# Making the low halves of the expert weights on GpSimd instead of VectorE

## The reference

```
h  = (qk * D / normalizer) v            # per head; D from running sums of log_sigmoid(fg) and ig
x  = x + head_norm(h) * out_w
s  = top2(softmax(layernorm(x) @ gate_w))
x  = x + sum_k s_k * (gelu(xf @ w1[e_k] + b1) @ w2[e_k] + b2)
```

## Time and profile before

| | before |
|---|---|
| time, median of 3 runs | 666.69 us (665.88 to 667.96) |
| profiled execution, span | 672.2 us |
| PE busy | 626.9 us (93%) |
| DVE busy | 489.8 us (73%) |
| ACT busy | 323.3 us (48%) |
| POOL (GpSimd) busy | 187.1 us (28%) |

### The profile page before, as it was taken

One profiled execution on the slowest core, in us unless ns is written; L12 is line 12 of the kernel. 1 busy time (PEld: TensorE's weight loads), 2 busy tenths in 40 slices (PEclk: granted clock), 3 DMA queues, 4 the chain that ended last, 5 costly groups with the idle time before them and its releaser, 6 DMA issues. The chain is left out here.

```text
span 672.2 us, 20373 instructions
## 1 busy us (share of the span) xinstructions
PE 626.9 (93%) x6736; PEld 533.2 (79%) x6737; DVE 489.8 (73%) x1330; ACT 323.3 (48%) x767; POOL 187.1 (28%) x185
## 2 busy tenths in 40 slices
PE   1799998999889899999999999999999999999985
PEld 1567876778677668988989898988889898988774
DVE  2457988979889898985889866757675757666562
ACT  2668888777878746543332232323232323232321
POOL 3000003231323315135345332313141323233112
PEclk9899999969999999999999999999999999999998
DMA  4534537654644636333374423233232323133100
GB/s 139 156 106 148 160 94 231 188 189 144 207 152 137 199 103 208 77 70 78 66 221 93 68 40 61 43 56 46 46 52 44 57 39 64 35 65 53 21 4 1
DMA packets 55036, 66.55 MB, mean 99 GB/s; under 512 B 5472, under 2 KB 50720, under 8 KB 54832
## 3 DMA queue, kind: packets, MB, share of 16 engines
q1 hardware_dynamic: 41552, 48.13, 24.1%
q0 software_dynamic: 13296, 17.32, 14.1%
q10 hardware_dynamic: 112, 0.08, 0.1%
HBM read 41.50 MB, written 24.92 MB: 99 GB/s over the span
## 5 line engine op out<-in xcount | busy, mean ns | idle before, releaser
L1038 ACT ACTIVATE decay_slots<-scores,b_turned 128x256 f32<-128x256 f32 (+1 forms) x312 | 124.4, 451 | 257.4 <-PE scores L1519 244.9
L1519 PE MATMUL scores<-x_slots,w_halves 128*128 128x256 f16 (+1 forms) x1872 | 203.3, 264 | 0.8 <-issue 0.8
L1519 PEld LDWEIGHTS scores<-x_slots,w_halves 128*128 x1872 | 173.4, 98 | 23.3 <-issue 1.4
L641 POOL DMA_INDIRECT expert_rows<-xf_rows,slot_i x64 | 66.7, 1042 | 224.1 <-issue 114.8
L1533 PE MATMUL pv<-w_halves,decay_slots 128*128 x864 | 97.7, 273 | 0.0
L663 POOL DMA_INDIRECT out_rows<-v_centred_and_one,row_ids x36 | 57.8, 1605 | 138.8 <-DVE v_centred_and_one L2111 96.1
L1533 PE MATMUL gate_bank<-w_halves,q_and_k_halves 128*128 x840 | 95.0, 273 | 0.0
L1533 PEld LDWEIGHTS pv<-w_halves,decay_slots 128*128 128x128 f16 x864 | 84.1, 98 | 10.5 <-issue 0.3
L1533 PEld LDWEIGHTS gate_bank<-w_halves,q_and_k_halves 128*128 128x128 f16 x840 | 81.8, 98 | 10.1
L663 POOL DMA_INDIRECT out_rows<-work,row_ids x35 | 55.3, 1580 | 112.1 <-DVE work L2111 84.7
L1257 PEld LDWEIGHTS pv<-v_centred_and_one,decay_slots 128*128 128x128 f32 x512 | 64.5, 197 | 1.6
(11 more groups left out here) (257 smaller groups left out, 845.5 us busy)
## 6 DMA issues: line engine op xcount, KB each, us to landing
weight_stage<-in_L_ffn_w SPq DMA_DIRECT2D x32, 512.0 KB
x_slots<-in_x SPq DMA_DIRECT2D x16, 512.0 KB
weight_stage<-expert_rows SPq DMA_DIRECT2D x30, 272.0 KB
ctx_slots<-in_ctx SPq DMA_DIRECT2D x8, 512.0 KB
out_rows<-x_slots SPq DMA_DIRECT2D x8, 512.0 KB
v_centred_and_one<-expert_rows SPq DMA_DIRECT2D x9, 272.0 KB
expert_rows<-v_centred_and_one SPq DMA_DIRECT2D x9, 272.0 KB
expert_rows<-xf_rows,slot_i POOLq DMA_INDIRECT x64
```

What stands on the lines that cost most here:

```text
L641: pool.indirect_dma_start(table, bass.IndirectOffsetOnAxis(ap=sloti[:, step[1], j, k:k + 1], axis=0), xfn[:, step[1], j, :], None, bounds_ ...
L1038: ins = act.activation(hf[:, f * R:f * R + tr.rows(0)], ps_s[:, q, n * R:n * R + tr.rows(0)], ACT.Gelu, bias=b1T[:, bass.ds(expert, 1), f] ...
L1519: ins = pe.matmul(o, w, xh[:, tr.slot(0) % 2, b, k, 0:tr.rows(0)], start=(n == 0), stop=(n == 3 * KC - 1))
```

## The change

All 32 low halves move from DVE to GpSimd. There a piece takes two instructions: the slot of the stage is multiplied by 64 in place, and, after a wait on a new semaphore for that, the high half is subtracted from it. The semaphore of low halves becomes two, one for each slot of the stage, and SP's loads wait for the one of their slot. The twelve pieces of S0 to S2 stand at the start of GpSimd's list. In a round its list is now: low half 0 of `nxt`, the preparation and the first pair of the scatter of the step before `last`, low half 1, two pairs, low half 2, the last pair, low half 3. So each scatter begins one round later than it did. The scatter of S5 follows behind the loop. DVE's list loses its calls of `weights_low` and is otherwise as it was.

```diff
-        s_lo = sem("weights_low")
+        s_w64 = sem("weights_scaled")
+        s_lo = [sem(f"weights_low{p}") for p in range(2)]
...
-                        sp.wait_ge(s_lo, g * 4 + (n - 1))
+                        sp.wait_ge(s_lo[half], g * 2 + q)
...
-                sp.wait_ge(s_lo, 4 * NSTEP)
+                for done in s_lo:
+                    sp.wait_ge(done, 2 * NSTEP)
...
+                def weights_low(step, n):
+                    g, half, q = number(step), n % 2, n // 2
+                    pool.wait_ge(s_hi, g * 4 + n + 1)
...
+                    src = stage[:, half, :]
+                    pool.tensor_scalar(src, src, W_SCALE, None, ALU.mult).then_inc(s_w64, 1)
+                    pool.wait_ge(s_w64, g * 4 + (n + 1))
+                    pool.tensor_tensor(lo, src, hi, ALU.subtract).then_inc(s_lo[half], 1)
...
                 def body(last, step, nxt, after):
-                    if last is not None:
-                        scatter(last)
+                    older = divmod(number(last) - 1, 2)
+                    weights_low(nxt, 0)
+                    scatter_ready(older)
+                    scatter_row(older, 0)
+                    weights_low(nxt, 1)
+                    scatter_row(older, 1)
+                    scatter_row(older, 2)
+                    weights_low(nxt, 2)
+                    scatter_row(older, 3)
+                    weights_low(nxt, 3)
 
                 def first_steps():
-                    scatter(S0)
+                    for step in (S0, S1, S2):
+                        for n in range(4):
+                            weights_low(step, n)
 
                 first_steps()
                 run_steps(body, pool)
+                scatter(divmod(NSTEP - 3, 2))
...
-                    dve.scalar_tensor_tensor(out=lo, in0=stage[:, half, :], scalar=W_SCALE, in1=hi, op0=ALU.mult,
-                                             op1=ALU.subtract).then_inc(s_lo, 1)
```

More of the change, by code:

```diff
@@ L621, in _, with scatter_row, scatter_ready @@
                     pool.memset(xfn[:, p, :, D:ROW], 0.0).then_inc(s_cp, 1)
-                def scatter(step):
+                def weights_low(step, n):
+                    g, half, q = number(step), n % 2, n // 2
+                    pool.wait_ge(s_hi, g * 4 + n + 1)
+                    e, k = g, q
+                    if half == 0:
+                        hi, lo = (w1s[:, bass.ds(e, 1), a, k, :].rearrange("p a f -> p (a f)") for a in range(2))
+                    else:
+                        hi, lo = (w2s[:, bass.ds(e, 1), a, k * (FC // 2):(k + 1) * (FC // 2), :].rearrange("p a c d -> p (a c d)")
+                                  for a in range(2))
+                    src = stage[:, half, :]
+                    pool.tensor_scalar(src, src, W_SCALE, None, ALU.mult).then_inc(s_w64, 1)
+                    pool.wait_ge(s_w64, g * 4 + (n + 1))
+                    pool.tensor_tensor(lo, src, hi, ALU.subtract).then_inc(s_lo[half], 1)
+                def scatter_row(step, j):
+                    for k in range(2):
+                        if j:
+                            pool.wait_ge(s_sc[step[1]][k], step[0] * SCATTERED + j * 16)
+                            pool.sem_inc(s_held, 1)
+                        pool.indirect_dma_start(
+                            table, bass.IndirectOffsetOnAxis(ap=sloti[:, step[1], j, k:k + 1], axis=0),
+                            xfn[:, step[1], j, :], None, bounds_check=TABLE - 1,
+                            oob_is_err=False).then_inc(s_sc[step[1]][k], 16)
+                def scatter_ready(step):
                     g = number(step)
@@ L635, in scatter @@
                     pool.sem_inc(s_held, 1)
+                def scatter(step):
+                    scatter_ready(step)
                     for j in range(SB):
[L637 to L644, removed]
-                def body(last, step, nxt, after):
-                    if last is not None:
-                        scatter(last)
+                        scatter_row(step, j)
+                def body(last, step, nxt, after):
+                    older = divmod(number(last) - 1, 2)
[8 more added lines that the diff above has]
+                    weights_low(nxt, 3)
                 def first_steps():
-                    scatter(S0)
+                    for step in (S0, S1, S2):
+                        for n in range(4):
+                            weights_low(step, n)
                 first_steps()
                 run_steps(body, pool)
+                scatter(divmod(NSTEP - 3, 2))
                 def add_rows(tr):
@@ L1887, in body @@
                         next_stats(after)
-                    if nxt is not None:
-                        weights_low(nxt, 0)
                     if after is not None:
@@ L1895, in body @@
                         next_a(nxt)
-                        weights_low(nxt, 1)
                         running_max(nxt)
@@ L1901, in body @@
                         h_norm(step)
-                    if nxt is not None:
-                        weights_low(nxt, 2)
                     if step is not None:
@@ L1918, in body @@
                         c_of(nxt, 1)
-                        weights_low(nxt, 3)
                     if nxt is not None and after is None:
@@ L1931, in first_steps @@
                     next_norm(S0)
-                    weights_low(S0, 0)
                     constants()
-                    weights_low(S0, 1)
                     gate_bias(S0)
@@ L1941, in first_steps @@
                     split(S0)
-                    weights_low(S0, 2)
                     max_log_decay(S0)
@@ L1945, in first_steps @@
                     next_stats(S2)
-                    weights_low(S0, 3)
                     c_of(S0, 1)
                     gate_bias(S1)
-                    weights_low(S1, 0)
                     next_norm(S2)
@@ L1954, in first_steps @@
                     c_of(S0, 3)
-                    weights_low(S1, 1)
                     running_max(S1)
                     split(S1)
-                    weights_low(S1, 2)
                     max_log_decay(S1)
@@ L1965, in first_steps @@
                     gate_bias(S2)
-                    weights_low(S1, 3)
                     x1_stats(S0)
@@ L1969, in first_steps @@
                     x1_norm(S0)
-                    weights_low(S2, 0)
                     log_f(S2)
@@ L1978, in first_steps @@
                     split(S2)
-                    weights_low(S2, 1)
-                    weights_low(S2, 2)
                     h_norm(S1)
@@ L1990, in first_steps @@
                     c_of(S2, 1)
-                    weights_low(S2, 3)
                     log_f(S3)
```

## The result

| | before | after |
|---|---|---|
| time, median | 666.72 us (665.88 to 667.96) | 721.39 us (720.30 to 723.07) |
| ratio, 95% interval | | 1.0824 [1.0785, 1.0864] |
| profiled execution, span | 672.2 us | 718.2 us |
| busy PE / DVE / ACT / POOL | 626.9 / 489.8 / 323.3 / 187.1 us | 661.6 / 502.4 / 326.0 / 349.0 us |

Ratios and their intervals here compare the runs within 1.5% of the fastest of each kernel; medians and ranges are of all its runs.

A forecast was written before the change was run, and what follows sets the result against it. No single engine bounds the attention rounds: TensorE and VectorE are both close to full. 8.0 us from five rounds plus 1.5 from 40 to 100 us give +9.5 on the median 666.69: 676 us, range 657 to 691.

The forecast's parts named there:

- Removed from DVE: Attention rounds: four DVE instructions fewer a round, each moving its successor by 1.14 us, give DVE 4.6 us a round.
- the rival: No hold on DVE: pieces run beside it in the rounds, time 660, at best 656; chance 25%.
- The holds on DVE: In the rounds, DVE's two-SBUF-input instructions wait for GpSimd's reading instructions to end: 6.6 us a round lost.
- the overlay: One round's two-input DVE instructions laid against GpSimd's four pieces: losses 2.5, 1.15, about 2.7 and 0 to 0.5 us.
- What of it reaches PE: Share of DVE's lateness passed to PE in the rounds: 1.6 us a round, 8.0 over five rounds.
- 2.5 us of slack swallow it: Low 2's net delay of 1.55 us at the next step's c_of is absorbed before PE wants it; 0.25 let through.
- A few us come on top: If PE idles more and its clock drops again (0.95), a few us beyond the forecast's own range 670 to 684.
- The scaling at 1.05 us: GpSimd's in-place scaling of a 128x1024 fp32 piece, from the affine selects' slope: 1.05 us of a 3.25 us piece.
- GpSimd becomes the bound: Rival: pieces above 3.9 us make low halves and loads late in the rounds; at 4.9 us +24, 691; chance 10%.
- From 3.9 us a piece on it does not: GpSimd's room in a 30 us round: 27.6 us used at most, 0.6 us spare a piece, too little from 3.9 us.
- The hand-over at nothing: End of the last round: last pieces end about 245, first tile's load issues at 247.52; 2.5 us spare, no cost.
- The late scatters at nothing: Row scatters one round later in GpSimd's list: records long ready, first tiles need only five early steps; priced at nothing.

The follow-up runs named there:

- e3: Changed kernel with GpSimd's two instructions per piece replaced by two memsets (1.9 us, nothing read, low halves zero): 656.13 us, 0.9835 of the kernel before.
- e2: Changed kernel without the scaling: GpSimd only subtracts, 2.2 us a piece, low halves wrong numbers: 713.18 us, 1.0688 of the kernel before.
- e15: Changed kernel with two memsets per piece (low halves zero), and without the filler matmuls that PE already had: 680.01 us, 1.0252 of the kernel before.
- e8: Changed kernel with additional filler matmuls on PE in every round: 721.47 us, 1.0853 of the kernel before.
- e4: Kernel before, low halves still on DVE, with only the scatters one round later: 667.92 us, 0.9995 of the kernel before.
- e1: Changed kernel with GpSimd's two instructions per piece replaced by five memsets (4.8 us, nothing read, low halves zero): 705.22 us, 1.0578 of the kernel before.

## Why the prediction was wrong

- **Removed from DVE: right.** 32 pieces of 1.22 us; without reads and with short pieces the kernel gains 11 us (e3), and the rival had put 7 to 11.
- **The holds on DVE: right in kind, and near in size partly by luck.** They were inferred from rows 9 in the other direction. By the rule of the Trainium skill, SBUF — State Buffer, section "Who interferes with whom", a two-input instruction of DVE had to be held by the subtraction, and the trace agrees now in both directions. 6.6 us a round was the overlay's sum; 1.6 us for each of the 32 pieces is 6.4 us a round. But the two sums hold different things. The two-input products grew by 38 us, 4.8 a round. The overlay missed that one-input instructions are held too: the cast L1711 took 1.05 us in the mean instead of 0.32, and L1642, with four numbers a partition, 0.70. And its 2.5 us for low 0 contradict its own rows: the removal of the low half at 158.42 brings the records 1.14 us forward, so L1820 is done by 161.4, ahead of low 0 at 161.5. In the changed kernel it was low 3 that held the records (L1834 at 175.28).
- **What of it reaches PE: wrong, and this step fails by itself, without the dear scaling: e2 lost 57 us against e3.** I let 1.6 us a round through. With holds alone a round costs 33.9 - 26.2 = 7.7 us (e2's last rounds), 4.0 of them idle time of PE. "2.5 us of slack swallow it" took low 2's hold as 1.55 us net and the only one in that chain, and put low 3 beside `c_of` at 0 to 0.5 (passing over `x1_of`, L1757, which also runs there and has both inputs in SBUF). But low 3, one scatter pair behind low 2, falls into the same chain, which then ends 4.5 us late: more than the slack, for PE at its scores and for ACT at `exp_f`. What I added per piece had to be added per chain.
- **"A few us come on top" for the clock: wrong, and the largest size.** In the five rounds of the changed kernel PE idles 6.8 us more and is 26.0 us longer busy with the same matmuls, at 0.70 to 0.95 instead of 0.84 to 1.00. That a fall of the clock costs time without any engine being later is shown in e15, but for this stretch not in this size. Idle time of PE was what I priced; each idle us came, in e2's rounds, with another 0.9 us of slower matmuls (3.7 to 4.0), and in the changed kernel with 3.8 (26.0 to 6.8). What of the 26 us would come back if only the clock were kept up in the changed kernel itself stays open: in e8 PE's busy time fell by 9.9 us and the time did not.
- **The scaling at 1.05 us: wrong.** 2.80 us, beyond the slope of the affine selects. A piece of 5.0 us meets the condition that the rival "GpSimd becomes the bound" named (4.9), at 10%.
- **"From 3.9 us a piece on it does not" fit: wrong.** I measured the room against rounds of 30 us, which held the very waits and the slow clock; an undisturbed round is 26.2. With the same 8.3 us of issues and 6.3 of landings the room is at most (26.2 - 14.6) / 4 = 2.9 us a piece, worked out afterwards. At 1.9 us the kernel gains 11 us, at 2.9 us nothing is left of it, and from there on every us costs 20 (666, 686, 705). The price of +24 at 4.9 us was too low as well: without a read 4.8 us gave +38.
- **The hand-over at nothing: wrong, and not for the reason that I had named.** The last pieces do end late, and the first tile's load waits for them, 3.6 us where it was 1.7, and before that for a scatter, 5.4 us. But PE did not wait for this load: it takes the first tile's rows up (L1538) without idle time, and what it did wait for, some us earlier, was DVE:
```profile
289.94 0.51 PE L1234 MATMUL scores<-q_and_k_halves 32*128 32x128 f16 x24 [2.48 <-DVE decay_slots L1735]
...
295.28 1.09 PE L1538 MATMUL turn_bank<-ident,weight_stage 128*128 128x128 f32 x4
```
From the first `c_of` of S7 to the first GELU, before and then changed:
```profile
238.50:261.02 22.52, 21.93 (x262) 17.67 (x261) 19.85 (x69) 10.13 (x24) 4.66 (x6) 1.00 0.55 179
```
```profile
276.40:308.75 32.35, 28.62 (x257) 23.20 (x258) 24.21 (x68) 9.64 (x22) 18.14 (x14) 0.74 0.44 146
```
Of the 9.8 us, 6.7 are PE itself at a clock of 0.74 instead of 1.00, and 3.1 are idle time. Most of these, the 2.48 us, ended with one `c_of` (L1735), behind the list of the first tiles, in which the last piece held L1873, 13 numbers a partition, for 2.12 us:
```profile
286.14 2.12 DVE L1873 TENSOR_SCALAR ctx_slots<-ctx_slots 128x13 f32<-128x13 f32 x1
```
- **The late scatters at nothing: right** (e4).

The sum does not split into shares of two causes: reads alone (e2) and five memsets (e1) each make PE idle in most rounds, and the clock falls with either. That the two don't add fits this, but no run separates it further.

## What to carry to other kernels

Work moved to an idle engine is not free because that engine is idle: compare its round with the undisturbed round of the kernel, not with today's mean, and ask of each instruction that the other engine holds who waits for it in order, not only who takes its nearest product. On a kernel that lives on PE, put a price on the clock: an idle us of PE came here with 0.9 to 3.8 us of slower matmuls. If two engines must share reads, placing the shorter instruction beside one whose second input lies in PSUM takes most of the loss away (701 to 680); with a fourth of the pieces of each round back on DVE (667) the kernel only comes back to where it was.

## What the runs showed of the hardware

- On GpSimd a multiplication of 128x1024 fp32 by a constant takes 2.77 us, longer than a product of two fp32 tiles (2.34) and 2.7 times a copy (1.04); output type and place made no difference.
- Beside a GpSimd instruction that reads SBUF, DVE's products of 0.16 to 0.19 us took up to 2.87, and one-input casts up to 1.98. Beside memsets, which read nothing, the two-input products nearly all kept their lengths (2 us of growth in e1); casts and other small one-input instructions still grew, 21 us in all (the cast of `slot_i` from at most 0.27 to 0.93 us).
- Rounds of the same 375 matmuls lay at 25.98 us of PE's time at a clock of 1.00, 29.7 at 0.85 and 36.5 at 0.70, within one kernel or between kernels.
